# Expert loop: list marks made three experts ahead behind the row evictions, and the product of SiLU and up kept in PSUM for both of its parts

## The chip, the cores and the metric

The kernel runs on one core of one Trainium2 chip. The metric is the time of one execution in device microseconds (us). The kernel before took 2899.19 us (median of three runs, 2895.27 to 2901.91).

The engines are named as in the profile: PE is TensorE (PEld its weight loads), DVE is VectorE, ACT is ScalarE, POOL is GpSimd, SP is SyncE. L2154 is line 2154 of the kernel.

## The reference

Two layers, each of a gated cross-attention and a gated feed-forward part, over x of shape (2, 512, 512). The change touches the feed-forward part of layer 0, a mixture of 16 experts, of which each of the 1024 tokens takes 4:

```python
def _L0_ffn_ref(x, ln_w, ff_ln_w, wq, wk, wv, wo, wg, w1, w3, w2):
    ...                                   # self-attention, x = x + o @ wo
    h = _rms(x, ff_ln_w)
    logits = h @ wg
    topv, topi = jax.lax.top_k(logits, TOP_K)          # TOP_K = 4 of E = 16
    gate = jax.nn.softmax(topv, -1)
    ...
    weights = jnp.zeros_like(logits).at[bidx, sidx, topi].set(gate)
    a = jax.nn.silu(jnp.einsum('bsd,edh->bseh', h, w1)) * jnp.einsum('bsd,edh->bseh', h, w3)
    y = jnp.einsum('bseh,ehd->bsed', a, w2)
    moe = jnp.einsum('bsed,bse->bsd', y, weights)
    return x + moe

x = x + jnp.tanh(g_xattn[0]) * _L0_xattn_ref(_layernorm(x), ctx_1024, ...)
x = x + jnp.tanh(g_ffn[0]) * _L0_ffn_ref(_layernorm(x), ...)
x = x + jnp.tanh(g_xattn[1]) * _L1_xattn_ref(_layernorm(x), ctx_1024, ...)
x = x + jnp.tanh(g_ffn[1]) * _L1_ffn_ref(_layernorm(x), ...)
```

All of w1, w3 and w2 of an expert are 512 by 512, in float32.

## The kernel before

The expert stage (`experts()`, L1720 on) lies at about 1709 to 2205 us of the span. It has two versions; with these inputs the one named `few_...` runs, which works on lists: of an expert's tokens at most CAP = 320 are taken, in CT = 3 rows of 128 places.

Every float32 operand is split in two parts, high (ACT copies it into the matmul's format) and low (the exact value minus the high part), and each product is three matmuls (high-high, low-high, high-low; `ACCURATE`). For the weights, ACT makes the high part (L1774) and POOL the low part (L1808), for w2, w1 and w3 in turn, from two buffers `e_raw` that SP fills by DMA (L1751). For activations ACT makes the high part and DVE the low part.

An expert e, with s = e % 2, is this on TensorE:

- L2154, 96 matmuls in four groups m: gate into `GU[m % 2]` columns 0 on, up into its columns from BANK on. `GU` is two pairs of PSUM banks, so group m + 2 writes where group m was.
- L2125, `order(e + 2)`: 24 small matmuls of the marks of expert e + 2 with the token records; they give the list of that expert's tokens in PSUM.
- L2135, `turn(e + 1, ...)`: transposes of the gathered rows of the next expert (chunks 0 and 1, then 2 and 3 after the first row of L2172).
- L2172: 36 matmuls with w2, for the rows r = 0, 1, 2 of places, into `Y`.

DVE, for each m, multiplies silu and up into `act32` in SBUF (L2095). ACT copies that as the high half `aT0[0]` (L1943), DVE subtracts for the low half `aT0[1]` (L2089). Between the two stand some of the marks of expert e + 2 (L2043): each compares the 384 place numbers of `count_up` with the place of a tile's token, three behind m = 0, three behind m = 1, two behind m = 2 (`MARKS`). There are eight tiles of tokens, so eight marks, and one buffer `mine` for them, which `order` reads. Then DVE computes where the results go (`targets`), reads the next list (`listed`), makes low halves of the next expert's tokens (L2071, `tokens`), and evicts the three rows of `Y` times the gate (L2104).

POOL gathers the rows of expert e + 1 by three indirect DMAs (L1985) at the start of an expert, and adds the results of expert e − 1 to DRAM by three indirect DMAs (L1996), in among the three low parts of weights.

Nothing but the program order of each engine and its semaphores sets the order. Those that matter: `s_mine` (marks, awaited by L2125), `s_a` (product), `s_ah` and `s_al` (high and low half), `s_list` (an order is done, so `mine` may be written), `s_yd` (a row is evicted). The PE group m waits on `s_a` until the product of group m − 2 is there. `s_al` begins at 2.

Of the kernel before, what the change touches and what calls it, by code (L numbers as in the profile page):

```python
# [7 lines left out]
P = 128  # L8
BANK = 512
F32 = mybir.dt.float32  # L10
# [5 lines left out]
ACT = mybir.ActivationFunctionType  # L16
# [5 lines left out]
NT = T // P  # L22
# [26 lines left out]
def program(nc, a, out):  # L49
    ctx = ExitStack()  # L50
    with ctx:
# [119 lines left out]
        def sb(name, shape, dt=F32):  # L171
            return phase.enter_context(nc.sbuf_tensor(name, shape, dt))
# [1031 lines left out]
        NE, TOPK, HID = 16, 4, 512  # L1204
        HC = HID // P
# [4 lines left out]
        CAP = T * TOPK // NE * 5 // 4  # L1210
        CT = -(-CAP // P)
        PLACES = CT * P
        place = sb("m_place", [P, NE + 2, NT])
        crowded = sb("m_crowded", [P, 1], I32)
        moe = {}
        h_rows = nc.dram_tensor("h_rows", (T, D), F32, kind="Internal").ap()
# [490 lines left out]
        def experts():  # L1707
# [7 lines left out]
            silu = [sb(f"e_silu{i}", [P, BANK]) for i in range(2)]  # L1715
            act32 = [sb(f"e_act{i}", [P, BANK]) for i in range(2)]
# [207 lines left out]
            def few_scalar(act):  # L1924
                for x in aT0:
                    rest = x[:, :, CAP:PLACES]
                    act.activation(rest, scrap[:, 63:64].unsqueeze(2).to_broadcast(list(rest.shape)), ACT.Copy)
                high(act, w1[0][0], 16, 0)
                high(act, w3[0][0], 16, 1)

                def tokens(e, s):
                    for c in range(KC):
                        act.wait_ge(s_xt, KC * e + c + 1)
                        act.activation(XS[s][0][:, c, :], TR[c % 2][:, 0:CAP], ACT.Copy).then_inc(s_xh, 1)

                tokens(0, 0)

                def body(i, s, last):
                    e = i * 2 + s

                    def part_high(m):
                        act.wait_ge(s_a, HC * (e + 1) + m + 1)
                        act.activation(aT0[0][:, m, 0:CAP], act32[m % 2][:, 0:CAP], ACT.Copy).then_inc(s_ah, 1)  # L1943

                    def next_high(w, k):

                        n = 3 * s + k
                        high(act, w[1 - s][0], 16 * (3 * i + 1 + n // 2 + 1), n % 2)

                    act.wait_ge(s_y, CT * (e + 1))  # L1950
                    high(act, w2[0], 16 * (3 * i + (1 if s == 0 else 3)) + (0 if s else 16), s)
                    for m in range(HC):
                        act.wait_ge(s_gu, HC * (e + 1) + m + 1)
                        act.activation(silu[m % 2][:, 0:CAP], GU[m % 2][:, 0:CAP], ACT.Silu).then_inc(s_sg, 1)
                        part_high(m)
                        if not last and m == 1:
                            next_high(w1, m)
                    if not last:
                        next_high(w3, 2)
                    tokens(e + 1, 1 - s)  # L1960

                def silu_table():
                    act.activation(scrap[:, 50:51], eps[:, 0:1], ACT.Silu)

                with act.Fori(0, NE // 2 - 1) as i:
                    silu_table()
                    for s in range(2):
                        body(i, s, False)
                silu_table()
                body(NE // 2 - 1, 0, False)  # L1970
                body(NE // 2 - 1, 1, True)
# [58 lines left out]
            def few_vector(dve):  # L2030

                dve.memset(scrap[:, 44:45], 0.0).then_inc(s_a, HC)
                dve.memset(scrap[:, 45:46], 0.0).then_inc(s_yd, CT)
                dve.memset(scrap[:, 46:47], 0.0).then_inc(s_al, 2)
                flat = place[:, :, :].rearrange("p e t -> p (e t)")

                def mark(e, tiles=range(NT)):

                    if not (isinstance(e, int) and e == 0):
                        dve.wait_ge(s_list, e)  # L2040
                    for t in tiles:
                        col = flat[:, t + e * NT:t + e * NT + 1] if isinstance(e, int) else flat[:, bass.ds(e * NT + t, 1)]
                        dve.tensor_scalar(mine[:, t, :], count_up[:, :], col, None, ALU.is_equal).then_inc(s_mine, 1)  # L2043

                def listed(e, s):
                    dve.wait_ge(s_list, e + 1)
                    found = Y[0][:, 0:6 * CT].rearrange("p (r k) -> p r k", k=6)
                    dve.tensor_copy(lists[s][:, :, :], found).then_inc(s_id, 1)
                    dve.tensor_reduce(ids32[:, :], found[:, :, 0:2], AX.X, ALU.add).then_inc(s_id, 1)
                    dve.wait_ge(s_id, LIST * e + 2)  # L2050
                    dve.tensor_copy(ids[s][:, :], ids32[:, :]).then_inc(s_id, 1)

                def targets(e, s):

                    dve.wait_ge(s_id, LIST * e + 1)
                    if not (isinstance(e, int) and e < 2):
                        dve.wait_ge(s_sum, 16 * CT * (e - 1))
                    dve.tensor_reduce(share[s][:, :], lists[s][:, :, 3:6], AX.X, ALU.add).then_inc(s_tg, 1)
                    dve.tensor_reduce(target32[0][:, :], lists[s][:, :, 0:2], AX.X, ALU.add).then_inc(s_tg, 1)
                    dve.tensor_tensor(target32[1][:, :], lists[s][:, :, 2], dummy[:, :], ALU.mult).then_inc(s_tg, 1)  # L2060
                    dve.wait_ge(s_tg, TARGET * e + 3)
                    dve.tensor_tensor(target32[0][:, :], target32[0][:, :], target32[1][:, :], ALU.subtract).then_inc(s_tg, 1)
                    dve.wait_ge(s_tg, TARGET * e + 4)
                    dve.tensor_tensor(target32[0][:, :], target32[0][:, :], dummy[:, :], ALU.add).then_inc(s_tg, 1)
                    dve.wait_ge(s_tg, TARGET * e + 5)
                    dve.tensor_copy(target[s][:, :], target32[0][:, :]).then_inc(s_tg, 1)

                def tokens(e, s):
                    for c in range(KC):
                        dve.wait_ge(s_xh, KC * e + c + 1)  # L2070
                        dve.tensor_tensor(XS[s][1][:, c, :], TR[c % 2][:, 0:CAP], XS[s][0][:, c, :].bitcast(F32),  # L2071
                                          ALU.subtract).then_inc(s_xl, 1)

                dve.wait_ge(s_up, 16)
                dve.wait_ge(s_ysum, 16)
                mark(0)
                listed(0, 0)
                mark(1)
                listed(1, 1)
                tokens(0, 0)  # L2080

                MARKS = (0, 3, 6, NT, NT)

                def body(i, s):
                    e = i * 2 + s

                    def part_low(m):
                        dve.wait_ge(s_ah, HC * e + m + 1)
                        dve.tensor_tensor(aT0[1][:, m, 0:CAP], act32[m % 2][:, 0:CAP], aT0[0][:, m, 0:CAP].bitcast(F32),  # L2089
                                          ALU.subtract).then_inc(s_al, 1)  # L2090

                    for m in range(HC):
                        dve.wait_ge(s_al, HC * e + m + 1)
                        dve.wait_ge(s_sg, HC * e + m + 1)
                        dve.tensor_tensor(act32[m % 2][:, 0:CAP], silu[m % 2][:, 0:CAP], GU[m % 2][:, BANK:BANK + CAP],  # L2095
                                          ALU.mult).then_inc(s_a, 1)
                        mark(e + 2, range(MARKS[m], MARKS[m + 1]))
                        part_low(m)
                    targets(e, s)
                    listed(e + 2, s)  # L2100
                    tokens(e + 1, 1 - s)
                    for r in range(CT):
                        dve.wait_ge(s_y, CT * (e + 1) + r + 1)
                        dve.tensor_scalar(y3[:, CT * s + r, :], Y[(r + 1) % 2][:, :], share[s][:, r:r + 1], None, ALU.mult).then_inc(s_yd, 1)  # L2104

                for s in range(2):
                    body(0, s)
                with dve.Fori(1, NE // 2) as i:
                    for s in range(2):
                        body(i, s)  # L2110
                dve.memset(scrap[:, 51:52], 0.0).then_inc(s_freed, 1)

            def few_tensor(pe):
# [29 lines left out]
                def body(i, s):  # L2143
# [1 line left out]
                    pe.wait_ge(s_lo, 3 * e + 1)  # L2145
                    pe.wait_ge(s_xl, KC * (e + 1))
                    for m in range(HC):
                        pe.wait_ge(s_a, HC * (e + 1) + m - 1)
                        for j, w in enumerate((w1[s], w3[s])):
                            if j and m == 0:  # L2150
                                pe.wait_ge(s_lo, 3 * e + 2)
# [865 lines left out]
```

## Time and profile before

| | us |
|---|---|
| median of three runs | 2899.19 (2895.27 to 2901.91) |
| the profiled execution | 2897.7 |
| its span, first to last instruction | 2895.9 |
| PE busy | 2411.6 (83%) |
| DVE busy | 1781.1 (62%) |
| ACT busy | 1482.8 (51%) |
| POOL busy | 1160.3 (40%) |

The profile is of one execution. Its span is 1.8 us shorter than the time of that same execution, which is 1.5 us below the median. Busy shares are means over stages of different kinds; the change touches only one, of about 470 us, so the rows below are of that stage. In the chain of work that ended last, L2154 has 5%, L2172 5%, and the marks L2043 2% of the span.

### The profile page before, as it was taken

How to read it: one execution, taken by the hardware profiler on the slowest of the kernel's cores; microseconds unless marked ns; L12 is line 12 of the kernel's file. 1: busy time of each engine (PE TensorE's matmuls, PEld its weight loads, DVE VectorE, ACT ScalarE, POOL GpSimd, SP SyncE). 2: the span in 40 equal slices, each digit the busy share in tenths (PEclk: the TensorE clock that was granted, in tenths of full speed). 3: DMA queues.
4: the chain of work that ended last, by engine and by line, in shares of the span. 5: the costliest groups of instructions: out<-in, count | busy, mean ns of one | idle time of the engine just before them, and what ended most of it. 6: DMA issues, size and time to landing. Idle time of an engine off the chain costs nothing. (4 is left out here: it accounts for less than half of the span.)

```text
span 2895.9 us, 46257 instructions
## 1 busy us (share of the span) xinstructions
PE 2411.6 (83%) x14790; PEld 2004.4 (69%) x14790; DVE 1781.1 (62%) x3865; ACT 1482.8 (51%) x3037; POOL 1160.3 (40%) x1561
## 2 busy tenths in 40 slices
PE   6999999999975998889885749999994698899365
PEld 3778787878864888888874538888883576677232
DVE  2555555555544666666665626565655787788576
ACT  3444444444435666666663443344332776777543
POOL 0222222222222444444442467787771544444000
PEclk9999999999996999999996969999997899999778
DMA  3000000000001000000003465665556332321100
GB/s 110 19 12 18 7 18 11 14 11 18 0 1 40 19 19 18 18 18 18 8 11 122 156 227 151 174 167 165 162 148 167 90 93 63 95 76 66 76 8 22
DMA packets 123653, 190.90 MB, mean 66 GB/s; under 512 B 18273, under 2 KB 66657, under 8 KB 121761
## 3 DMA queue, kind: packets, MB, share of 16 engines
q1 hardware_dynamic: 111408, 161.69, 18.3%
q0 software_dynamic: 10992, 25.96, 4.0%
q10 hardware_dynamic: 1152, 2.10, 0.3%
q8 instruction: 41, 0.67, 0.1%
q14 instruction: 60, 0.48, 0.1%
HBM read 143.58 MB, written 46.14 MB: 66 GB/s over the span
## 5 line engine op out<-in xcount | busy, mean ns | idle before, releaser
L435 ACT ACTIVATE x_p<-x_p,x_least 128x1024 f32<-128x1024 f32 x128 | 147.3, 1151 | 307.5 <-DVE x_least L391 307.5
L1808 POOL TENSOR_TENSOR e_w<-e_raw,e_w 128x2048 fp32r<-128x2048 f32 x48 | 222.0, 4627 | 70.5 <-ACT e_w L1774 70.4
L469 POOL TENSOR_TENSOR x_carry<-x_rtotal 128x1 f32<-128x1 f32 x128 | 24.7, 193 | 560.0 <-DVE x_rtotal L368 560.0
L375 DVE TENSOR_TENSOR x_pT<-pair,x_pT 128x512 fp32r<-128x512 f32 x256 | 164.4, 684 | 122.4 <-ACT x_pT L454 122.4
L2154 PE MATMUL pair<-m_h,e_w 128*128 128x320 f32 x1536 | 230.4, 311 | 1.1 <-DVE m_h L2071 1.1
L2154 PEld LDWEIGHTS pair<-m_h,e_w 128*128 128x128 f32 x1536 | 229.0, 190 | 2.9 <-issue 1.5
L537 PE MATMUL pair<-x_pT,x_v 128*128 128x256 f32 x1536 | 209.6, 293 | 9.2 <-DVE x_pT L375 9.2
L537 PEld LDWEIGHTS pair<-x_pT,x_v 128*128 128x128 f32 x1536 | 194.0, 194 | 26.3 <-issue 18.3
L565 PE MATMUL pair<-x_kT,x_qT 128*128 128x512 f32 x768 | 207.1, 405 | 0.0
L993 ACT ACTIVATE s_p<-s_p,s_least 128x128 f32<-128x128 f32 (+3 forms) x256 | 143.6, 561 | 123.4 <-DVE s_least L903 123.4
L2497 DVE TENSOR_REDUCE z_most<-pair 128x1 f32<-128x1008 f32 x128 | 154.0, 1203 | 73.4 <-PE pair L2607 51.2
L1131 PE MATMUL pair<-s_pT,s_v 128*128 128x256 f32 (+1 forms) x1152 | 158.3, 284 | 47.6 <-DVE s_pT L880 47.6
L1131 PEld LDWEIGHTS pair<-s_pT,s_v 128*128 128x128 f32 x1152 | 152.7, 195 | 60.1 <-issue 30.8
L2519 ACT ACTIVATE z_pT<-pair 128x512 fp32r<-128x512 f32 x256 | 141.7, 601 | 95.7 <-PE pair L2568 82.8
L1053 POOL TENSOR_TENSOR s_carry<-s_rtotal 128x1 f32<-128x1 f32 x256 | 49.6, 194 | 346.8 <-DVE s_rtotal L874 346.5
L2568 PE MATMUL pair<-ident,z_p 128*128 128x128 f32 x1024 | 144.6, 281 | 51.0 <-DVE z_pT L2490 49.9
L2533 ACT ACTIVATE z_p<-pair,z_most 128x1008 f32<-128x1008 f32 (+1 forms) x256 | 174.3, 696 | 12.5 <-DVE z_most L2498 12.5
L2568 PEld LDWEIGHTS pair<-ident,z_p 128*128 128x128 f32 x1024 | 117.1, 142 | 90.4 <-DVE z_pT L2490 61.8
L880 DVE TENSOR_TENSOR s_pT<-pair,s_pT 128x128 fp32r<-128x128 f32 (+3 forms) x256 | 124.7, 487 | 81.1 <-ACT s_pT L979 81.1
L2553 POOL TENSOR_SCALAR z_p<-z_p,z_rtotal 128x1008 f32<-128x1008 f32 (+1 forms) x256 | 174.6, 695 | 0.0
L2490 DVE TENSOR_TENSOR z_pT<-pair,z_pT 128x512 fp32r<-128x512 f32 x256 | 163.1, 679 | 4.5 <-ACT z_pT L2519 3.8
L454 ACT ACTIVATE x_pT<-pair 128x512 fp32r<-128x512 f32 x256 | 138.3, 594 | 45.0 <-PE pair L523 45.0
(336 smaller groups left out, 6189.9 us busy)
## 6 DMA issues: line engine op xcount, KB each, us to landing
e_raw<-in_L_ffn_w SPq DMA_DIRECT2D x48, 1024.0 KB
z_v<-z_vst SPq DMA_DIRECT2D x16, 768.0 KB, 3.6
z_kS<-z_k SPq DMA_DIRECT2D x24, 512.0 KB, 10.6
z_vS<-z_v SPq DMA_DIRECT2D x8, 1536.0 KB, 6.5
f_raw<-in_L_ffn_w SPq DMA_DIRECT2D x2, 4096.0 KB, 13.4
z_qS<-z_q SPq DMA_DIRECT2D x24, 256.0 KB, 4.5
s_wraw<-in_L_ffn_wq SPq DMA_DIRECT2D x9, 512.0 KB, 4.4
x_wq<-in_L_xattn_Wq SPq DMA_DIRECT2D x8, 512.0 KB, 3.6
```

Of the source, the lines that this page charges most:

```text
L375: dve.tensor_tensor(pT[1][:, keys, q * P:(q + 1) * P], TR[j][:, :].rearrange("p (k n) -> p k n", n=P), pT[0][:, keys, q * P:(q + 1) * P].b ...
L435: act.activation(p[n][:, :], p[n][:, :], ACT.Exp, scale=-1.0, bias=least[:, n:n + 1], accum_out=total[:, n:n + 1]).then_inc(s_ex, 1)
L537: mm = pe.matmul(OB[:, cols], v[x0][b][:, k, :], pT[x1][:, k, cols], start=(half == 0 and n == 0 and k == 0), stop=(half == 1 and n == 2 a ...
L565: mm = pe.matmul(SC[n % 2][:, j * BANK:(j + 1) * BANK], qT[x0][b][n // QT][:, n % QT * P:(n % QT + 1) * P], kT[x1][b][:, j * BANK:(j + 1) ...
L1131: mm = pe.matmul(OB[:, cols], v[b][:, k, first:first + 2, :].rearrange("p k d -> p (k d)"), pT[x1][:, k, cols], start=(i % 2 == 0 and half ...
L1808: pool.tensor_tensor(dst[1][:, :, :], raw[parity][:, :, :], dst[0][:, :, :].bitcast(F32), ALU.subtract).then_inc(s_lo, 1)
L2154: mm = pe.matmul(GU[m % 2][:, j * BANK:j * BANK + CAP], w[x0][:, c, m * P:(m + 1) * P], XS[s][x1][:, c, :], start=(n == 0 and c == 0), sto ...
L2490: dve.tensor_tensor(pT[1][:, k, cols], TR[i][:, :].rearrange("p (k n) -> p k n", n=P), pT[0][:, k, cols].bitcast(F32), ALU.subtract).then_ ...
L2497: dve.tensor_reduce(most[:, w, 0:1], SC[n % 2][:, 0:MAIN], AX.X, ALU.max, negate=True)
L2533: act.activation(p[w][:, cols], SC[n % 2][:, cols], ACT.Exp, bias=most[:, w, k:k + 1], accum_out=total[:, w, k:k + 1]).then_inc(s_ex, 1)
L2553: pool.tensor_scalar(p[w][:, cols], p[w][:, cols], rtotal[:, w, k:k + 1], 1.0, ALU.mult, ALU.mult).then_inc(s_pn, 1)
L2568: mm = pe.transpose(TR[i][:, k * P:(k + 1) * P], p[n % RING][:, kk * P:(kk + 1) * P], ident[:, :])
```

## The change

- `place`, the table of places, gets a column more for each tile, since marks are now made up to expert NE + 2 (the last ones are all zero and never read).
- The marks of expert e + 2 no longer stand between product and low half. Those of expert e + 3 are made behind the three row evictions of expert e, three, three and two. The marks of expert 2 are made at once before the loop.
- The product is written over the gate values in `GU` (PSUM), where ACT and DVE read it for both halves; `act32` in SBUF isn't used in this version of the loop.
- TensorE's group m waits on `s_al` for the low half of group m − 2, where it waited on `s_a` for its product. DVE's own wait on `s_al` ahead of the product goes.

```diff
@@ -1210,7 +1210,7 @@
         CAP = T * TOPK // NE * 5 // 4
         CT = -(-CAP // P)
         PLACES = CT * P
-        place = sb("m_place", [P, NE + 2, NT])
+        place = sb("m_place", [P, NE + 3, NT])
         crowded = sb("m_crowded", [P, 1], I32)
         moe = {}
         h_rows = nc.dram_tensor("h_rows", (T, D), F32, kind="Internal").ap()
@@ -1940,7 +1940,7 @@
 
                     def part_high(m):
                         act.wait_ge(s_a, HC * (e + 1) + m + 1)
-                        act.activation(aT0[0][:, m, 0:CAP], act32[m % 2][:, 0:CAP], ACT.Copy).then_inc(s_ah, 1)
+                        act.activation(aT0[0][:, m, 0:CAP], GU[m % 2][:, 0:CAP], ACT.Copy).then_inc(s_ah, 1)
 
                     def next_high(w, k):
 
@@ -2079,22 +2079,21 @@
                 listed(1, 1)
                 tokens(0, 0)
 
-                MARKS = (0, 3, 6, NT, NT)
+                MARKS = (0, 3, 6, NT)
+                mark(2)
 
                 def body(i, s):
                     e = i * 2 + s
 
                     def part_low(m):
                         dve.wait_ge(s_ah, HC * e + m + 1)
-                        dve.tensor_tensor(aT0[1][:, m, 0:CAP], act32[m % 2][:, 0:CAP], aT0[0][:, m, 0:CAP].bitcast(F32),
+                        dve.tensor_tensor(aT0[1][:, m, 0:CAP], GU[m % 2][:, 0:CAP], aT0[0][:, m, 0:CAP].bitcast(F32),
                                           ALU.subtract).then_inc(s_al, 1)
 
                     for m in range(HC):
-                        dve.wait_ge(s_al, HC * e + m + 1)
                         dve.wait_ge(s_sg, HC * e + m + 1)
-                        dve.tensor_tensor(act32[m % 2][:, 0:CAP], silu[m % 2][:, 0:CAP], GU[m % 2][:, BANK:BANK + CAP],
+                        dve.tensor_tensor(GU[m % 2][:, 0:CAP], silu[m % 2][:, 0:CAP], GU[m % 2][:, BANK:BANK + CAP],
                                           ALU.mult).then_inc(s_a, 1)
-                        mark(e + 2, range(MARKS[m], MARKS[m + 1]))
                         part_low(m)
                     targets(e, s)
                     listed(e + 2, s)
@@ -2102,6 +2101,7 @@
                     for r in range(CT):
                         dve.wait_ge(s_y, CT * (e + 1) + r + 1)
                         dve.tensor_scalar(y3[:, CT * s + r, :], Y[(r + 1) % 2][:, :], share[s][:, r:r + 1], None, ALU.mult).then_inc(s_yd, 1)
+                        mark(e + 3, range(MARKS[r], MARKS[r + 1]))
 
                 for s in range(2):
                     body(0, s)
@@ -2145,7 +2145,7 @@
                     pe.wait_ge(s_lo, 3 * e + 1)
                     pe.wait_ge(s_xl, KC * (e + 1))
                     for m in range(HC):
-                        pe.wait_ge(s_a, HC * (e + 1) + m - 1)
+                        pe.wait_ge(s_al, HC * e + m + 1)
                         for j, w in enumerate((w1[s], w3[s])):
                             if j and m == 0:
                                 pe.wait_ge(s_lo, 3 * e + 2)
```

On DVE, this is what stands in a row for expert 1 in the kernel before, from the reading of the next list on; `e_mine` are the marks, `e_act` the product in SBUF, `y` a row eviction:

```order
L2051 CAST e_ids<-e_ids 128x3
L2071 TENSOR_TENSOR m_h<-pair,m_h 128x320 x4
L2104 TENSOR_SCALAR y<-pair,e_share 128x512 x3
L2095 TENSOR_TENSOR e_act<-e_silu,pair 128x320
L2043 TENSOR_SCALAR e_mine<-e_count_up,m_place 128x384 x3
L2089 TENSOR_TENSOR e_aT<-e_act,e_aT 128x320
L2095 TENSOR_TENSOR e_act<-e_silu,pair 128x320
L2043 TENSOR_SCALAR e_mine<-e_count_up,m_place 128x384 x3
L2089 TENSOR_TENSOR e_aT<-e_act,e_aT 128x320
L2095 TENSOR_TENSOR e_act<-e_silu,pair 128x320
L2043 TENSOR_SCALAR e_mine<-e_count_up,m_place 128x384 x2
L2089 TENSOR_TENSOR e_aT<-e_act,e_aT 128x320
```

The same place in the changed kernel, where `pair` as the first name is the product in PSUM:

```order
L2051 CAST e_ids<-e_ids 128x3
L2071 TENSOR_TENSOR m_h<-pair,m_h 128x320 x4
L2103 TENSOR_SCALAR y<-pair,e_share 128x512
L2043 TENSOR_SCALAR e_mine<-e_count_up,m_place 128x384 x3
L2103 TENSOR_SCALAR y<-pair,e_share 128x512
L2043 TENSOR_SCALAR e_mine<-e_count_up,m_place 128x384 x3
L2103 TENSOR_SCALAR y<-pair,e_share 128x512
L2043 TENSOR_SCALAR e_mine<-e_count_up,m_place 128x384 x2
L2095 TENSOR_TENSOR pair<-e_silu,pair 128x320
L2090 TENSOR_TENSOR e_aT<-pair,e_aT 128x320
L2095 TENSOR_TENSOR pair<-e_silu,pair 128x320
L2090 TENSOR_TENSOR e_aT<-pair,e_aT 128x320
```

The eight marks have left the stretch of products and low halves and stand ahead of it, in among the evictions.

On TensorE, the head of an expert's gate and up matmuls in the loop, with the semaphores awaited, in the kernel before:

```order
L2154 MATMUL pair<-m_h,e_w 128x320 [waits e_a]
L2154 MATMUL pair<-m_h,e_w 128x320 x11
L2151 REGISTER_ALU
L2154 MATMUL pair<-m_h,e_w 128x320 [waits e_lo]
L2154 MATMUL pair<-m_h,e_w 128x320 x11
L2154 MATMUL pair<-m_h,e_w 128x320 [waits e_a]
L2154 MATMUL pair<-m_h,e_w 128x320 x23
```

And in the changed kernel:

```order
L2154 MATMUL pair<-m_h,e_w 128x320 [waits e_al]
L2154 MATMUL pair<-m_h,e_w 128x320 x11
L2151 REGISTER_ALU
L2154 MATMUL pair<-m_h,e_w 128x320 [waits e_lo]
L2154 MATMUL pair<-m_h,e_w 128x320 x11
L2148 REGISTER_ALU
L2154 MATMUL pair<-m_h,e_w 128x320 [waits e_al]
L2154 MATMUL pair<-m_h,e_w 128x320 x23
```

No matmul moves; the wait in front of each group is on the low half instead of the product.

## Rows read from the trace of the kernel before

**Rows 1.** Waits, expert loop: waiter, its releaser, us in total, times, longest.
```profile
POOL e_w L1808 <- ACT e_w L1774: 70.4, 38, 4.1
...
PE pair L2125 <- DVE e_mine L2043: 43.3, 17, 8.7
```

**Rows 2.** Timeline of TensorE: start, us, line, count, idle time before and its releaser.
```profile
1730.69 16.71 PE L2154 MATMUL pair<-m_h,e_w 128*128 128x320 f32 x96 [1.13 <-DVE m_h L2071]
...
1904.37 14.24 PE L2154 MATMUL pair<-m_h,e_w 128*128 128x320 f32 x96
...
1920.88 1.47 PE L2125 MATMUL pair<-e_token,e_mine 128*128 x24 [2.27 <-DVE e_mine L2043]
...
1922.81 3.05 PE L2172 MATMUL pair<-e_w,e_aT 128*128 128x512 f32 x12
...
1931.96 14.24 PE L2154 MATMUL pair<-m_h,e_w 128*128 128x320 f32 x96
...
1961.03 14.24 PE L2154 MATMUL pair<-m_h,e_w 128*128 128x320 f32 x96
...
2157.33 14.24 PE L2154 MATMUL pair<-m_h,e_w 128*128 128x320 f32 x96
...
2171.42 0.76 PE L2125 MATMUL pair<-e_token,e_mine 128*128 x24
...
2172.65 3.06 PE L2172 MATMUL pair<-e_w,e_aT 128*128 128x512 f32 x12
...
2175.54 0.82 PE L2135 MATMUL pair<-ident,e_rows 128*128 128x128 f32 x6
...
2176.11 5.84 PE L2172 MATMUL pair<-e_w,e_aT 128*128 128x512 f32 x24
```

**Rows 3.** Windows: busy times (instructions), granted clock, DMA share, GB/s.
```profile
1932.10:1961.20 29.10, 26.89 (x171) 24.33 (x170) 16.98 (x32) 11.95 (x17) 23.92 (x16) 0.94 0.62 185
...
1952.00:1954.00 2.00, 2.00 (x6) 1.53 (x5) 0.63 (x2) 0.03 (x1) 2.00 (x1) 0.50 1.11 285
...
2157.50:2182.00 24.50, 24.50 (x169) 22.38 (x168) 13.34 (x33) 6.98 (x13) 12.25 (x10) 1.00 0.40 59
```

**Rows 4.** Timeline of VectorE (DVE), the same columns.
```profile
1717.28 2.71 DVE L2043 TENSOR_SCALAR e_mine<-e_count_up,m_place 128x384 bf16<-128x384 f32 x8
...
1927.50 0.74 DVE L2104 TENSOR_SCALAR y<-pair,e_share 128x512 f32<-128x512 f32 x1
...
1943.89 4.38 DVE L2043 TENSOR_SCALAR e_mine<-e_count_up,m_place 128x384 bf16<-128x384 f32 x2
...
1951.74 0.89 DVE L2071 TENSOR_TENSOR m_h<-pair,m_h 128x320 fp32r<-128x320 f32 x2 [0.38 <-ACT m_h L1934]
```

**Rows 5.** Timeline of ScalarE (ACT), end of one expert.
```profile
1949.49 1.90 ACT L1774 ACTIVATE e_w<-e_raw 128x2048 fp32r<-128x2048 f32 x1
1951.29 0.74 ACT L1934 ACTIVATE m_h<-pair 128x320 fp32r<-128x320 f32 x2
```

**Rows 6.** Timeline of GpSimd (POOL), start-up and one expert.
```profile
1718.34 1.77 POOL L1985 DMA_INDIRECT e_rows<-h_rows,e_ids  x1 [0.60 <-issue]
...
1720.42 0.97 POOL L1985 DMA_INDIRECT e_rows<-h_rows,e_ids  x1 [0.30 <-issue]
...
1943.15 4.57 POOL L1808 TENSOR_TENSOR e_w<-e_raw,e_w 128x2048 fp32r<-128x2048 f32 x1 [1.99 <-ACT e_w L1774]
...
1951.47 4.56 POOL L1808 TENSOR_TENSOR e_w<-e_raw,e_w 128x2048 fp32r<-128x2048 f32 x1 [1.74 <-ACT e_w L1774]
```

**Rows 7.** Groups by line, expert loop: count | busy us, mean ns | idle before.
```profile
L2089 DVE TENSOR_TENSOR e_aT<-e_act,e_aT 128x320 fp32r<-128x320 f32 x64 | 31.0, 485 | 9.7 <-ACT e_aT L1943 9.7
...
L2095 DVE TENSOR_TENSOR e_act<-e_silu,pair 128x320 f32<-128x320 f32 x64 | 30.8, 482 | 80.2 <-ACT e_silu L1954 80.2
...
L1943 ACT ACTIVATE e_aT<-e_act 128x320 fp32r<-128x320 f32 x64 | 30.2, 473 | 71.3 <-DVE e_act L2095 71.3
...
L1954 ACT ACTIVATE e_silu<-pair 128x320 f32<-128x320 f32 x64 | 27.7, 434 | 89.3 <-PE pair L2154 89.3
```

## The prediction

> **What bounds the kernel now.** I read four views in this order. The view of waits comes first, over the expert loop: TensorE stands idle at L2125 until DVE's list marks are there, 17 times and 43.3 us in total [rows 1]; two of those are in the start-up before the loop (8.7 and 3.3 us), so 31.3 us are left inside it. The timeline of TensorE shows where: after the 96 gate and up matmuls (L2154) it waits 2.27 us, then runs the order matmuls L2125, and goes on [rows 2]. The starts of the sixteen L2154 groups, 1730.69 to 2157.33, give the time of an expert: 32.45 us for expert 0, seven of 28.7 to 29.1 (1931.96 to 1961.03 is one), seven of 27.2 to 27.6 (1904.37 to 1931.96 is one), whose mean is 27.41.
>
> The windows tell the two kinds apart: the expert from 1932.10 has a mean clock of 0.94, since the granted clock falls to 0.50 (1.2 GHz instead of 2.4) just behind the idle stretch [rows 3]. A slow expert costs about 1.5 us more.
>
> The timelines of DVE and POOL tell why the marks are late. They are 0.33 us each when nothing is in the way (eight in 2.71 us), but the two of the third group take 4.38 us from 1943.89, and POOL's low-half subtraction runs from 1943.15 for 4.57 us, to 1947.72 [rows 4, 6]. A mark that begins beside POOL's `e_w` subtraction ends about when that does.
>
> Expert 15 of this same trace is the picture of the loop without that wait. POOL has no w1 and w3 to do there, the marks are in time, and TensorE goes from L2154 to the order matmuls at once, 2171.42 being 14.09 us after 2157.33 [rows 2]. The x24 order group is followed after 1.23 us by L2172, against 1.93 us in the expert from 1904.37 (1920.88 to 1922.81, of which L2135 is the same 0.6 in both): with no wait in front, the register work of the order matmuls is hidden too. The expert is over at about 2181.8 (the last group's 5.84 us less the overlap of ends of 0.15), so it took 24.5 us, all at clock 1.00 [rows 2, 3].
>
> **The change part by part.**
>
> *Marks behind the row evictions.* Eight marks leave the path between L2154 and L2125, and are made an expert earlier. I take 24.5 us as the time of an expert without the wait: 27.41 − 24.5 = 2.9 us off, of which 2.2 is the wait and 0.7 the order group.
>
> Where do they go? In the expert that starts at 1931.96 the first eviction runs at 1927.50 to 1928.24, 3.7 us before it [rows 4]. POOL's w3 subtraction will then end about 2.7 us before the next start: ACT's w3 copy follows the last high half, 15.7 us behind the start, takes 1.9 us, and POOL takes 4.6. So the first three marks lose about a microsecond, the second eviction starts about 0.8 us late, and the last marks are over at about 2 us behind the next start. The next thing DVE is asked for is the first product, 4.1 us behind it. The late eviction is asked for by nobody until TensorE's next order group 14 us on. Cost: nothing; the cover is 2 us of DVE idle time, beyond which each microsecond would move the product.
>
> *What is late next.* The second pair of row transposes (L2135) needs the low halves of chunks 0 and 1 of the next tokens. ACT reaches those chunks after its last `e_w` copy, as now (1949.49 plus 1.90, then 1951.29), and DVE is done 1.34 us after ACT begins [rows 4, 5]. With silu 0.43, product 0.48, high half 0.47, three gaps of 0.1 and the copy of 1.9 [rows 7], ACT begins the tokens 17.5 us behind the start and DVE ends at 18.85. TensorE would come to these transposes at 18.2 and to chunk 3 at 18.5. I take a stall of 0.4 us: 24.9 us per expert. Bounds: 0 (as in expert 15) and 0.7.
>
> *Product in PSUM.* No instruction is added. DVE now writes PSUM; no row shows that. The nearest are its reads of PSUM: product 482 ns, token low half about 480 (0.89 us for two) [rows 4, 7]. I take 482, 473 and 485 ns for the three operations as they are. As to the lock with POOL: the product and the token low half have one input in PSUM and one in SBUF; the token pair at 1951.74 ran in 0.89 us beside the POOL subtraction that began at 1951.47 [rows 4, 6]. The new L2090 has the same kinds of input, so I take it as free of POOL. With the product in SBUF it would now fall beside POOL's work, which it never did before; that is a cost the trace doesn't show, avoided if my reading holds.
>
> In the Trainium skill (SBUF — State Buffer, "Who interferes with whom") a DVE instruction with two SBUF inputs contends with a GpSimd instruction that reads SBUF, and one with a single SBUF input outside the two-port modes doesn't. The 0.89 us agrees for the second half; no row here shows the first.
>
> *The new wait on low halves.* TensorE's group m now waits for low half m−2 rather than for the product. The chain behind a group's end is silu, product, high, low with gaps: 0.43 + 0.48 + 0.47 + 0.49 + 0.3 = 2.2 us, against 3.5 us (a quarter of 14.24) until the other buffer's group is over. Slack 1.3 us; cost nothing. Ahead of the last r = 0 matmuls, low half 3 comes 2.2 us behind L2154's end and is needed at 3.2.
>
> *Clock.* With the wait gone the low-activity stretch is about 1.2 us instead of 3.7. In expert 15 the clock stays at 1.00. I take the dips in experts 1 to 14 as gone: 7 × 1.5 = 10.5 us. Expert 0 has a dip of 2.5 that goes, and 2.5 at its beginning (16.71 against 14.24) that stays.
>
> *POOL's own pace.* POOL waits 70.4 us for ACT's copies over the loop [rows 1]. The first fifteen experts average (2157.33 − 1730.69)/15 = 28.4 us, so it needs about 28.4 − 70.4/15 = 23.8 us per expert. That is 1.1 below 24.9: just not the bound.
>
> *Start and end.* The eight extra marks before the loop fall between the last token low half and the first product (over 6 us), those after the last eviction beside the scatters' DMA. Nothing.
>
> **Sum.** Before: 426.6 + 24.5 = 451.1 us from the first L2154 to the loop's end. After: 27.4 (expert 0) + 14 × 24.9 + 24.5 = 400.5. The gain is 50.6 us, of which 37.7 wait, order group and new stall, and 13 clock. The profiled execution took 2897.7 us (its span 2895.9), 1.5 below the median of the runs; 2897.7 − 50.6 = 2847.1. Against the median it would be 2848.6; I say 2848.
>
> **The rivals.**
> A. POOL becomes the bound. The marks move right into the stretch in which POOL makes the descriptors of the gathers. In the start-up a gather that ran beside a row of marks took 1.77 us against 0.97 for the next, and ended at 1720.11, just behind the marks' end at 1719.99 [rows 4, 6]. For it: this number. Against: it is the very first gather, which may be slow for that alone. If POOL loses the full 8 × 0.33 = 2.6 us, it needs 26.4 us per expert: 14 × 1.5 = 21 us of the gain go, 2869. Partial loss beyond 1.1 us gives values between. 20%.
> The Trainium skill says in the same section that `tensor_scalar` can enter a two-port mode, and that whoever issues first keeps the shared pair for the whole instruction while the other blocks; by that rule the gathers would be held up.
> B. The dips of the clock stay, since the stretch of order matmuls and transposes remains: half of the experts at 1.5 us and expert 0's 2.5, 2848 + 13 = 2861. For it: the dips came in experts with the same work as others, so one clean expert 15 says little. 13%.
> C. Slower. DVE's write to PSUM, or reading it for both halves, is so slow that L2154 waits for low halves. Each of two waits (groups 2 and 3) costs what the chain takes beyond 3.5 us. To lose the 50.6 us, 3.4 per expert, the chain must be over 5.2 us, i.e. the three operations 4.5 us rather than 1.45; at 5.4 us it is 15 × 0.4 = 6 us slower than before, 2905. For it: no row of a DVE write to PSUM. Against: reads cost nothing extra. 3%.
> D. The change doesn't do what it says: marks stay stuck behind POOL in the new place, the last group past the 2 us of cover, and hold the first product; the wait at L2125 goes but half as much comes back ahead of L2154's third group, about 25 us: 2873. 4%.
>
> **Numbers.** The forecast has 60%, with 2842 to 2854 of its own (stall 0 to 0.7 is −6 to +4, and run to run about 2). The range 2840 to 2870 takes in B and A. No change can be told from under 0.2%, about 6 us. Faster 0.95, same 0.02, slower 0.03.
>
> **What would show it.** Right: no idle time in front of L2125 inside the loop; its group of 24 in about 0.8 us; L2154 to L2154 in about 24.9 us at clock 1.00, with a small wait of L2135 for L2071. Rival A: gathers L1985 of over 1.3 us and POOL hardly waiting for L1774. B: clock 0.5 behind L2125. C: L2154 idle on L2090. The forecast is wrong if the L2154 starts stay over 26 us apart.

## The result, and the profile after

The changed kernel takes 2850.68 us (median of six runs, 2847.69 to 2856.8) against 2900.6 us for the kernel before in six runs on the same chip: the ratio is 0.9832, with a 95% interval of 0.9821 to 0.9842. That is 49.9 us less; 2848 was forecast.

The head of the profile page of the changed kernel:

```profile
span 2851.2 us, 46210 instructions
## 1 busy us (share of the span) xinstructions
PE 2396.0 (84%) x14782; PEld 1993.0 (70%) x14790; DVE 1718.3 (60%) x3873; ACT 1483.3 (52%) x3037; POOL 1162.3 (41%) x1561
```

TensorE's timeline for one expert (start us, us, line, count, idle time before and its releaser), which answers to [rows 2]:

```profile
1937.81 14.24 PE L2154 MATMUL pair<-m_h,e_w 128*128 128x320 f32 x96
1951.89 0.76 PE L2125 MATMUL pair<-e_token,e_mine 128*128 x24
1952.51 0.85 PE L2135 MATMUL pair<-ident,e_rows 128*128 128x128 f32 x6
1953.12 3.04 PE L2172 MATMUL pair<-e_w,e_aT 128*128 128x512 f32 x12
1956.32 0.85 PE L2135 MATMUL pair<-ident,e_rows 128*128 128x128 f32 x6 [0.16 <-DVE m_h L2071]
1956.93 5.83 PE L2172 MATMUL pair<-e_w,e_aT 128*128 128x512 f32 x24
1962.61 14.24 PE L2154 MATMUL pair<-m_h,e_w 128*128 128x320 f32 x96
```

The idle 2.27 us in front of L2125 are gone, its 24 matmuls take 0.76 us instead of 1.47, and an expert takes 24.80 us. All fourteen from the second to the fifteenth take 24.79 to 24.81. What is left of idle time is 0.16 us in front of the second row transposes. The waits over experts 1 to 15 (waiter, releaser, us in total, times, longest) say the same:

```profile
ACT e_w L1774 <- PE pair L2172: 68.8, 15, 5.2
...
POOL e_w L1808 <- ACT e_w L1774: 13.4, 26, 0.6
...
PE pair L2135 <- DVE m_h L2071: 2.3, 14, 0.2
```

The window over the same stretch (columns as in [rows 3]: PE, PEld, DVE, ACT, POOL busy, granted clock, DMA share, GB/s) has TensorE busy for 369.7 of 372 us, at a mean granted clock of 1.00:

```profile
1764.00:2136.00 372.00, 369.70 (x2523) 338.69 (x2521) 186.57 (x481) 162.22 (x236) 326.97 (x193) 1.00 0.68 182
```

DVE's timeline in front of that expert shows where the marks went:

```profile
1933.35 0.74 DVE L2103 TENSOR_SCALAR y<-pair,e_share 128x512 f32<-128x512 f32 x1
1934.01 2.10 DVE L2043 TENSOR_SCALAR e_mine<-e_count_up,m_place 128x384 bf16<-128x384 f32 x3
1936.03 0.74 DVE L2103 TENSOR_SCALAR y<-pair,e_share 128x512 f32<-128x512 f32 x1
1936.69 1.06 DVE L2043 TENSOR_SCALAR e_mine<-e_count_up,m_place 128x384 bf16<-128x384 f32 x3
1938.01 0.75 DVE L2103 TENSOR_SCALAR y<-pair,e_share 128x512 f32<-128x512 f32 x1 [0.26 <-PE pair L2172]
1938.68 0.74 DVE L2043 TENSOR_SCALAR e_mine<-e_count_up,m_place 128x384 bf16<-128x384 f32 x2
1942.00 0.50 DVE L2095 TENSOR_TENSOR pair<-e_silu,pair 128x320 f32<-128x320 f32 x1 [2.58 <-ACT e_silu L1954]
```

And POOL beside it:

```profile
1930.62 4.62 POOL L1808 TENSOR_TENSOR e_w<-e_raw,e_w 128x2048 fp32r<-128x2048 f32 x1 [0.54 <-ACT e_w L1774]
1935.20 0.30 POOL L1983 TENSOR_TENSOR e_carry<-eps 128x1 f32<-128x1 f32 x1
1935.66 1.03 POOL L1985 DMA_INDIRECT e_rows<-h_rows,e_ids  x1 [0.16 <-issue]
1936.99 0.99 POOL L1985 DMA_INDIRECT e_rows<-h_rows,e_ids  x1 [0.30 <-issue]
...
1940.70 5.19 POOL L1808 TENSOR_TENSOR e_w<-e_raw,e_w 128x2048 fp32r<-128x2048 f32 x1
```

Only the first three lose a microsecond, to the end of POOL's w3 subtraction at 1935.24 (2.10 us instead of 1.06). The last two end at 1939.42, 1.6 us behind the expert's start and 1.3 us ahead of POOL's w2 subtraction, and 2.6 us of idle DVE time follow before the first product. The two groups of lines for the two halves (count | busy us, mean ns) answer to [rows 7]:

```profile
L2095 DVE TENSOR_TENSOR pair<-e_silu,pair 128x320 f32<-128x320 f32 x64 | 31.8, 497 | 139.5 <-ACT e_silu L1954 139.5
L2090 DVE TENSOR_TENSOR e_aT<-pair,e_aT 128x320 fp32r<-128x320 f32 x64 | 31.5, 492 | 32.3 <-ACT e_aT L1943 32.3
```

From the first L2154 to the end of the last L2172 the loop takes 399.5 us against 451.3: 51.8 less. In the profiled pair the whole gains only 44.7 (2897.7 to 2853.0), most of the rest being that the first L2154 starts at 1736.5 instead of 1730.7. Nothing that it waits for is changed but the width of one memset, and four of the kernels below, with the same code there, start the loop at 1731.2 to 1733.6 in their profiled executions. The six-run medians carry the statement, not the pair.

### The profile page after: what moved, and what is told of

The parts are those of the page before. It is cut to its first block and busy times, and to the rows that moved or that the text cites. A ratio compares the mean times of both kernels' runs of the same rounds, so it can differ in the third digit from the quotient of the medians.

```text
span 2851.2 us, 46210 instructions
## 1 busy us (share of the span) xinstructions
PE 2396.0 (84%) x14782; PEld 1993.0 (70%) x14790; DVE 1718.3 (60%) x3873; ACT 1483.3 (52%) x3037; POOL 1162.3 (41%) x1561
## 5 line engine op out<-in xcount | busy, mean ns | idle before, releaser
L1808 POOL TENSOR_TENSOR e_w<-e_raw,e_w 128x2048 fp32r<-128x2048 f32 x48 | 229.2, 4776 | 19.8 <-ACT e_w L1774 19.6
L2154 PE MATMUL pair<-m_h,e_w 128*128 128x320 f32 x1536 | 230.7, 311 | 1.1 <-DVE m_h L2071 1.1
L2154 PEld LDWEIGHTS pair<-m_h,e_w 128*128 128x128 f32 x1536 | 229.3, 190 | 2.9 <-issue 1.5
L2497 DVE TENSOR_REDUCE z_most<-pair 128x1 f32<-128x1008 f32 x128 | 154.0, 1203 | 70.6 <-PE pair L2607 49.9
```

What stands on the lines that cost most here:

```text
L1808: pool.tensor_tensor(dst[1][:, :, :], raw[parity][:, :, :], dst[0][:, :, :].bitcast(F32), ALU.subtract).then_inc(s_lo, 1)
L2154: mm = pe.matmul(GU[m % 2][:, j * BANK:j * BANK + CAP], w[x0][:, c, m * P:(m + 1) * P], XS[s][x1][:, c, :], start=(n == 0 and c == 0), sto ...
L2497: dve.tensor_reduce(most[:, w, 0:1], SC[n % 2][:, 0:MAIN], AX.X, ALU.max, negate=True)
```

## The experiments

The periods below are from the start of one L2154 group to the next, over experts 1 to 14 of the one profiled execution of each kernel. A dip is a stretch inside an expert in which the granted clock is 0.50 instead of 1.00. The runs of before on their chip have medians of 2900.94 us (first four) and 2901.28 us (last two).

**One half alone: marks moved, product in SBUF.** From the changed kernel:

```diff
-  act.activation(aT0[0][:, m, 0:CAP], GU[m % 2][:, 0:CAP], ACT.Copy).then_inc(s_ah, 1)
+  act.activation(aT0[0][:, m, 0:CAP], act32[m % 2][:, 0:CAP], ACT.Copy).then_inc(s_ah, 1)
-  dve.tensor_tensor(aT0[1][:, m, 0:CAP], GU[m % 2][:, 0:CAP], aT0[0]..., ALU.subtract)
+  dve.tensor_tensor(aT0[1][:, m, 0:CAP], act32[m % 2][:, 0:CAP], aT0[0]..., ALU.subtract)
+  dve.wait_ge(s_al, HC * e + m + 1)                                            # as before the change
-  dve.tensor_tensor(GU[m % 2][:, 0:CAP], silu..., ALU.mult).then_inc(s_a, 1)
+  dve.tensor_tensor(act32[m % 2][:, 0:CAP], silu..., ALU.mult).then_inc(s_a, 1)
-  pe.wait_ge(s_al, HC * e + m + 1)
+  pe.wait_ge(s_a, HC * (e + 1) + m - 1)
```

> One half of the change alone: the marks behind the row evictions, but the product of SiLU and up in SBUF as before, and TensorE's groups waiting on the product. My theory: the marks are nearly all of the gain, and the product in PSUM only keeps the low halves (two SBUF inputs each) out from behind POOL's subtraction. Low halves 0 and 2 will now last until POOL's e_w subtraction ends (2 to 3 us instead of 0.49), low half 3 comes about 0.7 us later, and an expert takes 25.2 to 25.8 us instead of 24.8: 2857 to 2868 us. Rival 1, the SBUF product is as good, since no row has shown a low half held up by POOL: 24.8 us per expert, 2850. Rival 2, the low halves cost as much as the marks did: no better than before, about 2895.

Measured: 2870.69 us, ratio 0.989 (0.9874 to 0.9905); 26.13 us per expert. DVE and then POOL in one expert:

```profile
1925.49 3.13 DVE L2090 TENSOR_TENSOR e_aT<-e_act,e_aT 128x320 fp32r<-128x320 f32 x1 [0.54 <-ACT e_aT L1943]
```

```profile
1923.10 5.17 POOL L1808 TENSOR_TENSOR e_w<-e_raw,e_w 128x2048 fp32r<-128x2048 f32 x1
```

The low half with both inputs in SBUF lasts until POOL's subtraction is over (1928.27). Of the 64 low halves, 31 do so; the mean of all is 1869 ns, the longest takes 3575. So neither rival holds: the held-up low half is real, and it costs 1.33 us per expert. That is over my upper bound of 1.0, and so is the time (2868 was the bound). TensorE shows where, twice per expert:

```profile
1936.44 3.03 PE L2173 MATMUL pair<-e_w,e_aT 128*128 128x512 f32 x12 [0.69 <-POOL e_w L1808]
1940.04 0.85 PE L2136 MATMUL pair<-ident,e_rows 128*128 128x128 f32 x6 [0.57 <-DVE m_h L2071]
```

The first of these names POOL as the releaser, whose w2 half had long been done; it is a wait for several semaphores, and in the expert before, low half 2 ended at 1910.21 and the same matmuls began at 1910.31.

**The other half alone: product in PSUM, marks in their old place.**

```diff
   dve.tensor_tensor(GU[m % 2][:, 0:CAP], silu..., ALU.mult).then_inc(s_a, 1)   # in PSUM, as in the change
+  mark(e + 2, range(MARKS[m], MARKS[m + 1]))                                   # where it was before
   part_low(m)
   ...
-  mark(e + 3, range(MARKS[r], MARKS[r + 1]))                                   # behind a row eviction
```

> The other half alone: product in PSUM and TensorE waiting on low halves, with the marks between product and low half as before. My theory: the marks' end is set by POOL's w1 subtraction, and that by ACT's copy of w1, neither of which moves; TensorE is held some 1.4 us at its third group by low half 0, and waits as much less in front of L2125. An expert takes as long as before, 27.4 to 28 us (28.4 with clock dips): 2890 to 2905. Rival, the product in PSUM is a gain of its own: under 2885.

Measured: 2896.2 us, ratio 0.9984 (0.9975 to 0.9993). As expected within the range: the idle time of one expert is split in two.

```profile
1908.86 7.30 PE L2153 MATMUL pair<-m_h,e_w 128*128 128x320 f32 x48 [1.24 <-DVE e_aT L2089]
1916.89 1.48 PE L2124 MATMUL pair<-e_token,e_mine 128*128 x24 [0.73 <-DVE e_mine L2043]
```

An expert with full clock takes 27.3 to 27.6 us, as before (27.50 on average, against 27.41). In the profiled executions what it gains is of the clock: two experts of fourteen have a dip (29.1 us) instead of seven. That the 4.7 us between the medians are the same thing is likely, not shown. Alone the halves give 30.3 and 4.7 us; together 49.9. The other 14.9 us come only with both, since each half alone leaves TensorE waits of over a microsecond per expert that the other one takes away.

**The idle stretch put back, without a stuck mark.**

```diff
   pe.wait_ge(s_yd, CT * (e + 1) - 1)
+  pe.wait_ge(s_al, HC * (e + 1) + 2)
   order(e + 2)
```

> The changed kernel, with one wait more on TensorE: the order matmuls wait for low half 3 of their expert, which comes 2.0 us behind L2154's end. This puts back an idle stretch like that of before at the same place, without any mark stuck behind POOL. My theory: of the 49.9 us that the change brought, the wait itself is 2.1 us per expert, the order group's hidden register work 0.7, and the rest, about 12 us, the clock, which fell behind the idle stretch. Expected: L2125 x24 in 1.46 us again, the clock at 0.5 for some microseconds in about half of the experts, 24.8 + 2.1 + 0.6 = 27.5 per expert without a dip, 2850 + 15 x 2.7 + 12 = 2902. Rival 1, the clock fell before for another reason (what DVE and POOL did): no dips, 2890. Rival 2, the register work was not shown by the wait: L2125 x24 stays at 0.76 us, 10 us less.

Measured: 2916.85 us, ratio 1.0052 (1.0037 to 1.0068), slower than the kernel before. One expert on TensorE, and the window of the loop:

```profile
1929.10 1.50 PE L2125 MATMUL pair<-e_token,e_mine 128*128 x24 [2.25 <-DVE e_aT L2090]
...
1931.63 3.79 PE L2173 MATMUL pair<-e_w,e_aT 128*128 128x512 f32 x12
```

```profile
1766.00:2172.50 406.50, 374.97 (x2341) 339.70 (x2341) 212.79 (x444) 157.73 (x223) 310.39 (x180) 0.93 0.60 159
```

Both rivals fall. The order group is back at 1.5 us behind a wait, and the clock is back at 0.5 for a stretch in every expert: the mean period is 29.24 us, against 24.80 + 2.25 + 0.74 − 0.16 = 27.6 without dips. The 1.6 us over that are the dip, the size of before. What I had wrong is how often, and with it the time (2902 expected): in every expert, where the kernel before, with 1.9 to 2.3 us of idle time, had it in seven of fourteen. The profiled execution is the slowest of the four, at 2924.13 us, so the others may have fewer or shorter dips.

**ACT makes two chunks of tokens ahead of its copy of w3.**

```diff
+  tokens(e + 1, 1 - s, range(2))
   if not last:
       next_high(w3, 2)
-  tokens(e + 1, 1 - s)
+  tokens(e + 1, 1 - s, range(2, KC))
```

> The changed kernel, with ACT making the high halves of token chunks 0 and 1 of the next expert before its copy of w3 instead of after it. In the changed kernel an expert takes 24.80 us, 0.33 above the 24.47 of expert 15, and TensorE waits 0.16 us each time in front of the second row transposes for DVE's low half of chunk 1. My theory: that wait is the copy of w3; with the tokens ahead of it an expert takes 24.47 us, POOL's w3 subtraction is 0.8 us later and still in time, and 15 x 0.33 = 5 us go: 2846. Rival, POOL (which has about 1.1 us to spare per expert) becomes the bound with its w3 input late: the same or some 5 us slower, 2850 to 2856.

Measured: 2841.74 us in five runs (2841.34 to 2843.26), ratio 0.9798 (0.9785 to 0.9812): the fastest version, clear of the changed kernel's interval. An expert takes 24.42 to 24.45 us, and the view of waits has no wait of TensorE left:

```profile
1928.04 14.24 PE L2155 MATMUL pair<-m_h,e_w 128*128 128x320 f32 x96
1942.12 0.76 PE L2126 MATMUL pair<-e_token,e_mine 128*128 x24
...
1943.35 3.04 PE L2173 MATMUL pair<-e_w,e_aT 128*128 128x512 f32 x12
1946.23 0.82 PE L2136 MATMUL pair<-ident,e_rows 128*128 128x128 f32 x6
1946.80 5.85 PE L2173 MATMUL pair<-e_w,e_aT 128*128 128x512 f32 x24
```

The time is better than the 2846 expected. Of the 8.9 us between this median and that of the changed kernel, the shorter experts explain 5.5 (15 × 0.37). In the profiled executions expert 0 is 1.9 us shorter too (25.8 against 27.7 us), as the clock comes up 2.8 us behind its start and not 6.2; it is 27.1 us where all marks follow the first eviction, so it differs between kernels that do the same there. Where the rest lies is not shown.

POOL waits for ACT 1.2 us in all over experts 1 to 15, against 13.4 in the changed kernel:

```profile
POOL e_w L1808 <- ACT e_w L1774: 1.2, 5, 0.3
```

So the wait that the change left is the w3 copy, as I took it. POOL all but never waits for ACT now; whether it would be the bound next isn't shown, as it still waits 10.6 us in all for the DMA of its scatters.

**All eight marks behind the last eviction.**

```diff
-  MARKS = (0, 3, 6, NT)
+  MARKS = (0, 0, 0, NT)
```

> The changed kernel, with all eight marks behind the third eviction instead of three, three and two behind the three. They then begin 0.9 us behind the next expert's start and need 2.7 us, while POOL begins its w2 subtraction 2.9 us behind it (for 4.6 us), and the first product is wanted at 4.2 us. My theory (rival D of the prediction as a mechanism): the last one or two marks get stuck until about 7.5 us, product 0 comes at 8 instead of 4.2, TensorE is held some 2.6 us in front of its third group, and the clock dips come back in some experts: 27.4 us per expert or more, 2885 to 2905. Rival 1: the marks all slip in ahead of POOL's subtraction, 24.8 us per expert, 2850. Rival 2: marks cost the same wherever they stand beside POOL, the distribution over the evictions doesn't matter: 2850 to 2860.

Measured: 2923.45 us, ratio 1.0082 (1.0062 to 1.0103): the same marks, one eviction or two later, turn a gain of 50 us into a loss of 22. DVE, POOL and TensorE in one expert (the last line is cut off by the end of the view):

```profile
1936.89 0.75 DVE L2103 TENSOR_SCALAR y<-pair,e_share 128x512 f32<-128x512 f32 x1 [2.05 <-PE pair L2172]
1937.56 8.27 DVE L2043 TENSOR_SCALAR e_mine<-e_count_up,m_place 128x384 bf16<-128x384 f32 x8
1945.75 0.48 DVE L2095 TENSOR_TENSOR pair<-e_silu,pair 128x320 f32<-128x320 f32 x1
```

```profile
1939.45 5.16 POOL L1808 TENSOR_TENSOR e_w<-e_raw,e_w 128x2048 fp32r<-128x2048 f32 x1
```

```profile
1936.69 7.20 PE L2154 MATMUL pair<-m_h,e_w 128*128 128x320 f32 x48
1947.28 7.96 PE L2154 MATMUL pair<-m_h,e_w 128*128 128x320 f32 x42 [3.39 <-DVE e_aT L2090]
```

The marks take 8.27 us instead of 2.7, the product comes 9 us behind the start instead of 4.2, and L2154's third group waits 3.4 us. A mean period of 29.9 us is more than the 27.4 expected, and the time is above the range of 2885 to 2905: the wait is 3.4 us rather than 2.6, and eleven experts of fourteen have a dip of the clock. The three without one take 28.4 to 28.5 us, 3.65 more than in the changed kernel, so the wait is most of the loss and the dips are the other 1.5 us of the mean. The order group, with no wait in front of it, takes 0.76 us here as in the changed kernel.

**All eight marks behind the first eviction.**

```diff
-  MARKS = (0, 3, 6, NT)
+  MARKS = (0, NT, NT, NT)
```

> The changed kernel, with all eight marks in one row behind the first eviction. They begin 3.8 us ahead of the next expert's start, are held by POOL's w3 subtraction until 2.6 us ahead of it, and then run in a row right beside POOL's first two gathers. If a row of marks holds up the making of a gather's descriptors until its end (rival A of the prediction, the 1.77 us of the first gather), the first gather of each expert takes 1.6 us or more instead of 1.03, and POOL, with 1.1 us to spare, about becomes the bound: 2850 to 2858. My theory after the trace of the changed kernel, in which gathers beside marks took 0.98 to 1.03 us: gathers stay at 1.0 us, nothing else waits for the two late evictions, 24.8 us per expert, 2850.

Measured: 2848.91 us, ratio 0.9825 (0.9803 to 0.9847), 24.80 us per expert. DVE's row of marks and POOL's gathers beside it:

```profile
1928.87 3.83 DVE L2043 TENSOR_SCALAR e_mine<-e_count_up,m_place 128x384 bf16<-128x384 f32 x8
```

```profile
1930.51 1.03 POOL L1985 DMA_INDIRECT e_rows<-h_rows,e_ids  x1 [0.16 <-issue]
1931.85 1.05 POOL L1985 DMA_INDIRECT e_rows<-h_rows,e_ids  x1 [0.30 <-issue]
```

The row ends at 1932.70; the first gather, wholly beside it, takes 1.03 us and the second 1.05. In the kernel before, with no mark beside them, the same two took this:

```profile
1928.84 1.03 POOL L1985 DMA_INDIRECT e_rows<-h_rows,e_ids  x1 [0.16 <-issue]
1930.18 0.98 POOL L1985 DMA_INDIRECT e_rows<-h_rows,e_ids  x1 [0.30 <-issue]
```

So the row of marks costs the gathers 0.1 us at most, and rival A falls.

## Why the prediction was right, point by point

*Marks off the path.* Right in mechanism and size. Experts at full clock went from 27.41 to 24.80 us, 2.61 each where 2.5 was taken. The order group's 0.7 us came as expert 15 had shown it; that it hangs on the wait in front is shown by the experiment that put the wait back (1.5 us again). What the wait uncovers stands in the last section.

*Where the marks go.* First marks held for about 1 us, the rest free, end 1.6 us behind the start (2 taken), no wait of TensorE for the late evictions. That the cover is what makes it free is shown by the row of eight behind the last eviction. Rival D was thus a real mechanism with the right place, though that kernel puts more marks there than D spoke of. Its price was far off: I gave it 25 us of a lost gain, and the measured version loses all of the gain and 22 us more, since the chain of product, high and low half is only started when the marks are through, and the clock falls too.

*What is late next.* The transposes behind the w3 copy, as forecast, but the sum named one chunk where two are late. The chain of work that ended last goes through chunk 0 (start, us, what):

```profile
1953.42 1.91 ACT e_w L1774
1955.33 0.34 ACT m_h L1934
...
1955.69 0.50 DVE m_h L2071
1956.19 0.14 issue
1956.32 0.85 PE pair L2135 x6
```

The transposes of chunk 2 wait for chunk 0's low half, which ends at 1956.18. Chunk 1's ends at 1956.57, just ahead of the transposes of chunk 3 at 1956.68, so it would have cost about as much alone; the sum took only this second one, 18.85 against 18.5. The stall was put at 0.4 us. It is 0.37, the difference between 24.80 and the 24.43 of the version that makes these chunks' high halves ahead of the w3 copy, which also shows that the copy is the reason. From the start of the first L2172 group to the transposes are 3.20 us in the changed kernel (1953.12 to 1956.32) and 2.88 there (1943.35 to 1946.23), so 0.32 late; the idle time that the timeline prints, 0.16, is only half of it. The ends of matmuls are modelled in a profile, which may be why.

*Product in PSUM.* Right. A DVE write to PSUM takes 497 ns against 482, the low half 492 against 485; ACT's read is 438 ns against 473. The claim that the second input in PSUM frees the low half of POOL was argued from L2071 and is now shown from both sides: 491 to 493 ns for all 64 with PSUM, up to 3575 with SBUF. In the changed kernel none of the L2154 groups waits on a low half.

*Clock.* Right: no dip in experts 1 to 14, and the experiment with the wait put back brings them back. The 10.5 us are the difference of counted experts. The prediction had one clean expert to go by, as rival B says, and when a given idle stretch brings a dip is still open (last section), so that none was left is in part luck.

*POOL's pace.* 23.8 us per expert was taken; at 24.43 us per expert POOL still waits 1.2 us in all for ACT's copies, so its own pace is no slower than that. Rival A is refuted for the gathers of the loop: those wholly beside back-to-back marks took 0.98 to 1.05 us. The 1.77 us were the very first gather. It took 1.77 in the changed kernel too, but there too it ran beside a row of marks; the fourth gather, also with marks beside it, took 0.98. That the first one is slow because it is the first is likely, not shown. The Trainium skill (SBUF — State Buffer, "Who interferes with whom") would have descriptor making held up by a DVE instruction in a two-port mode. No run here shows that; which mode the marks run in isn't shown either. What the same section says of two SBUF inputs, the run with the product in SBUF agrees with (3.13 us until POOL's subtraction ended).

*The sum.* 50.6 us forecast, 51.8 in the loop, 49.9 in the medians. In the loop, experts 1 to 14 give 36.5 us at full clock (35.1 forecast) and 10.5 us of dips, and expert 0 gives 4.8 (5.0 forecast), so the terms came out and not only their total. 2848 against 2850.7 is within run to run; from the six-run median of the kernel before, 2900.6, the same sum gives 2850.0.

## What to carry to other kernels

Look at what a DVE instruction that runs beside a long GpSimd one has as operands: `tensor_scalar` from SBUF to SBUF and `tensor_tensor` with two SBUF inputs lasted until the GpSimd instruction ended, and for `tensor_tensor` one input in PSUM was enough to be free of it. Where the work can't change form, move it beside GpSimd's indirect DMAs, which left the marks at 0.33 us each here, and check by the timeline that the last piece is through before the next long GpSimd instruction: a microsecond too late cost more here than the whole change had won. And look for an iteration in the trace that lacks the wait (here the last expert): its 24.5 us were within 0.3 us of what every expert but the first took afterwards.

## What the runs showed of the hardware that was not expected

- With an idle stretch of 2.25 us per expert in front of the order matmuls, the granted clock fell to 0.5 in fourteen experts of fourteen, and in the kernel before, whose stretch was 1.9 to 2.3 us, in seven. A longer stretch of 3.4 us inside the gate and up matmuls did it in eleven. With the idle time in two pieces of 1.24 and 0.73 us it fell in two of fourteen, with 0.69 and 0.57 us never. Each count is of one profiled execution. What tells the experts with a dip from those without stays open: in the kernel before, stretches of 1.91 and 2.25 us had one, and stretches of 1.92 and 2.27 us had none.
- The 24 order matmuls of an expert in the loop took 0.75 or 0.76 us with no wait in front and 1.45 to 1.52 us right behind one, whether the wait was 0.7 or 2.3 us long. The trace shows why. TensorE's sequencer runs eight register instructions among them, which compute the addresses of the token records. Behind a wait the first eight matmuls start 0.13 us apart, one for each of these, and the other sixteen 0.03 us apart. In the start-up the addresses are constants, no register instruction stands among the matmuls, and 24 of them took 0.80 and 0.78 us right behind waits of 8.7 and 3.3 us. A wait in front of such a group thus cost 0.7 us more than its idle time.
- Of the eight marks in one row behind the last eviction, the first took 0.54 us and the next three 0.33 each. The fifth began at 1939.08, 0.4 us ahead of POOL's subtraction by the profile's starts, and still lasted until 1944.84, just behind the subtraction's end at 1944.61; the last three ran at 0.33 us again. All fifteen experts from the second on show it, with the same 0.4 us. Spans on POOL are rough, so the true order of the two starts isn't certain, but a mark that begins shortly before the subtraction can be held by it.
